# A graph layer followed by routed experts, one core: the gate computed from rows that are not yet normalised, and a routing table of tile and lane numbers in bf16

## The reference, cut to what matters

```python
x = x + gnn(layernorm(x), ...)                 # 3125 rows of 256
x_flat = layernorm(x)
gate_logits = x_flat @ Wg + bg + bias          # 8 experts
topk_vals, topk_idx = top_k(gate_logits, 2)
topk_w = softmax(topk_vals)
h = relu(einsum('td,edh->teh', x_flat, W1) + b1)    # 256 -> 512
y = einsum('teh,ehd->ted', h, W2) + b2              # 512 -> 256
out = x + einsum('ted,te->td', y, combine)     # combine: the two weights in their experts' columns
```

## Time and profile before

| | us |
|---|---|
| median of 3 runs (1615.25 to 1617.7) | 1615.89 |
| the profiled execution's own time | 1618.14 |
| its span on the core | 1616.4 |
| TensorE busy in the span | 1404.1 |
| VectorE busy | 726.7 |
| GpSimd busy | 185.2 |

### The profile page before, as it was taken

How to read it: one execution, slowest core, us unless ns; L and a number is a source line. 1 busy time by engine, 2 the same in 40 slices (tenths; PEclk the granted TensorE clock), 3 DMA queues, 4 the chain that set the end, 5 groups by cost and what they waited for, 6 DMA issues and landing times.

```text
span 1616.4 us, 25299 instructions
## 1 busy us (share of the span) xinstructions
PE 1404.1 (87%) x8992; PEld 855.5 (53%) x8993; DVE 726.7 (45%) x1676; ACT 389.9 (24%) x1040; POOL 185.2 (11%) x156
## 2 busy tenths in 40 slices
PE   2565578898869999999999999999999953899996
PEld 1554344444434554447444554447444532899995
DVE  6989777777741432213131232214112266343342
ACT  1320254344330420103001130104001031244342
POOL 1000200000000000000000000000000002477774
PEclk9886779999989999999999999999999976899998
DMA  5244000000000000000000000000003092244443
GB/s 114 66 160 157 1 1 1 1 2 1 1 20 1 13 2 0 1 0 14 0 1 0 14 1 0 1 1 7 1 1 80 0 314 83 40 69 70 68 74 43
DMA packets 49431, 57.82 MB, mean 36 GB/s; under 512 B 14201, under 2 KB 41483, under 8 KB 49066
## 3 DMA queue, kind: packets, MB, share of 16 engines
q1 hardware_dynamic: 38570, 41.67, 8.6%
q0 software_dynamic: 10752, 14.69, 5.7%
HBM read 42.36 MB, written 13.99 MB: 35 GB/s over the span
## 4 chain that ended last, share of the span: by engine, by line
PE 77%; DVE 11%; ACT 4%; issue 3%; DVEq 1%; DMA 1%; POOL 1%; SPq 0%; POOLq 0%
PE bank L904 40%; PE bank L994 8%; PE bank L1452 6%; PE bank L1462 6%; PE bank L830 4%; PE bank L2059 3%; ACT at L1925 3%; PE bank L2001 2%; DVE ohL L1723 1%; PE bank L910 1%; PE bank L2057 1%; PE bank L1443 1%; ACT m L851 1%; DVE ohS L1832 1%; PE bank L1417 1%
## 5 line engine op out<-in xcount | busy, mean ns | idle before, releaser
L904 PE MATMUL bank<-at,m 125*128 125x500 fp8e4 (+1 forms) x3500 | 691.1, 355 | 11.7 <-DVE aggT L918 6.1
L904 PEld LDWEIGHTS bank<-at,m 125*128 125x128 f16 x3500 | 318.4, 98 | 374.9 <-issue 58.2
L920 DVE SCALAR_TENSOR_TENSOR aggT<-bank,dnL,dinvB 128x500 f32<-128x500 f32 (+1 forms) x56 | 38.2, 683 | 458.1 <-PE bank L910 458.1
L1452 PEld LDWEIGHTS bank<-xtT,w1c 128*128 128x128 f32 x896 | 109.8, 194 | 2.8
L1452 PE MATMUL bank<-xtT,w1c 128*128 128x128 f32 x896 | 110.0, 277 | 0.0
L1179 POOL TENSOR_TENSOR idJ<-idJ,wts 125x1400 f32<-125x1400 f32 x2 | 8.0, 4008 | 863.5 <-DVE idJ L1335 863.5
L1462 PE MATMUL bank<-w2s,h1T 128*128 x448 | 106.1, 380 | 0.1
L1195 POOL DMA_INDIRECT out_rows<-ytb,rowS x56 | 96.8, 1729 | 51.7 <-issue 24.3
L1462 PEld LDWEIGHTS bank<-w2s,h1T 128*128 128x128 f32 x448 | 80.8, 190 | 9.3 <-issue 0.3
L1016 ACT ACTIVATE hB<-aggT,prm 128x500 f32<-128x500 f32 (+1 forms) x28 | 18.7, 667 | 266.7 <-DVE aggT L1060 266.7
L2059 PE MATMUL bank<-cnt,ohS 128*128 128x250 bf16 x504 | 77.6, 302 | 0.0
(11 more groups left out here) (367 smaller groups left out, 1619.0 us busy)
## 6 DMA issues: line engine op xcount, KB each, us to landing
slrow<-sl_dram SPq DMA_DIRECT2D x26, 512.0 KB, 4.9
w1s<-in_L_ffn_W SPq DMA_DIRECT2D x1, 4096.0 KB, 14.5
w2s<-in_L_ffn_W SPq DMA_DIRECT2D x1, 4096.0 KB, 18.6
xin<-in_x SPq DMA_DIRECT2D x1, 2800.0 KB
out_rows<-x SPq DMA_DIRECT2D x1, 2800.0 KB
xn_dram<-xn SPq DMA_DIRECT2D x1, 2800.0 KB
x<-in_x SPq DMA_DIRECT2D x2, 1344.0 KB
dinvB<-dinv_dram SPq DMA_DIRECT2D x1, 1562.5 KB
```

The lines of the kernel that those rows point to most:

```text
L904: pe.matmul(agg_bank(l, g)[:, 0:w], m[:, s, k, h * 128:(h + 1) * 128], at_block(q)[:, s, :], start=s == 0 and k == 0, stop=False)
L1452: last = pe.matmul(bank[4 + u][:, k * TT:(k + 1) * TT], w1c[:, u, h, k * 128:(k + 1) * 128], xtT[:, u, h, :], start=h == 0, stop=h == H - 1)
```

## The change

It touches six things.

1. **Gate from x2.** TensorE transposes tiles of `x2`, before they are normalised, and multiplies each with `wgs`, now with the transposed tile as the stationary operand and the 8 columns of `wgs` moving. The logits come out with rows on partitions. Another matmul gives the column sums of `wgs` (`csW`). VectorE corrects the logits: (raw - mean * csW) * rstd + bias. The stream of TensorE waits for `s_fw` at its start.
2. **Statistics in halves.** `back_dve` adds four tiles in one instruction, and statistics are taken of each half of 128 elements. Those of the first half move to the last graph layer.
3. **xn by ScalarE.** ScalarE writes the normalised rows, with the softmax's exponential after the tenth. SyncE stores `xn` ahead of `x2`, in two DMAs.
4. **Slot table in bf16.** Lane (0 to 124) and 128 times the tile number, both exact in bf16, replace the row number. A third table holds plain ones, from which `used` tells which choice fills a slot. `xn_dram` has 128 rows for each tile of 125, so that tile and lane give the row directly.
5. **Weights with the rows.** A row of `xn` has 258 elements: 256 and the two softmax weights. After each gather VectorE picks the weight of the tile's slots by two operations of 128x1 (`select`), and the next gather into the buffer waits for it.
6. **Tile numbers by GpSimd.** `te` and `ts` are worked out in 13 GpSimd instructions instead of 8 of VectorE.

```diff
         def back_dve(dve, j, t):
...
-            dve.tensor_tensor(x2[:, t, part], x2[:, t, part], row_slot(j, t), ALU.add).then_inc(s_lo, 1)
+            n = set_of(t).stop - t
+            rows = bank[ROWS_AT + (j * SETS_T + t // PER) % 3][0:P, 0:n * 128].rearrange("p (t d) -> p t d", d=128)
+            dve.tensor_tensor(x2[:, set_of(t), part], x2[:, set_of(t), part], rows, ALU.add).then_inc(s_lo, n)
...
         def experts_sp(sp):
...
+            sp.wait_ge(s_wx, 1)
+            for a, b in X_STORES:
+                sp.wait_ge(s_fn, b)
+                sp.dma_start(xn_dram.rearrange("(t p) d -> p t d", p=TT)[:, a:b, :], xn[:, a:b, :]).then_inc(s_xnd, 16)
             sp.wait_ge(s_lo, NT * (L + 2))
...
         def experts_pool(pool, step):
...
-                step(pool.tensor_tensor(idJ[:, n, :, 1, :], byJ, wts[:, 2 - n, :].unsqueeze(2).to_broadcast([P, NT, J]), ALU.mult))
-                pool.tensor_tensor(byJ, byJ, iotaN[:, :].unsqueeze(2).to_broadcast([P, NT, J]), ALU.mult).then_inc(s_tabP, 1)
+            pool.memset(xn[96:TT, :, :], 0.0).then_inc(s_cst, 1)
+            pool.wait_ge(s_ends, 1)
+            done_at, before_at = cmpJ[:, 0, :, :], cmpJ[:, 1, :, :]
+            step(pool.tensor_tensor(done_at, nte[0:1, 2, :].unsqueeze(1).to_broadcast([1, J, NE]),
+                                    iotaJ[0:1, :].unsqueeze(2).to_broadcast([1, J, NE]), ALU.subtract))
+            step(pool.tensor_scalar(done_at, done_at, 0.5, None, ALU.is_lt))
+            step(pool.tensor_tensor(before_at, done_at, nte[0:1, 1, :].unsqueeze(1).to_broadcast([1, J, NE]), ALU.mult))
+            for n in (4, 2):
+                step(pool.tensor_tensor(cmpJ[:, :, :, 0:n], cmpJ[:, :, :, 0:n], cmpJ[:, :, :, n:2 * n], ALU.add))
...
+            pool.tensor_scalar(te[:, :], teF[:, :], float(NE - 1), None, ALU.min).then_inc(s_slot, 1)
...
                     pool.wait_ge(s_xtT, j + 1)
+                    pool.wait_ge(s_sel, j + 1)
                     gather(j + XB)
...
         def experts_act(act):
...
+                act.activation(turned_x(t), bank[t % 4][:, 0:H * P].rearrange("p (h n) -> p h n", h=H), ACT.Copy).then_inc(s_gTe, 1)
...
+                if t == EXP_AT:
+                    act.wait_ge(s_ex, 1)
+                    act.activation(wts[:, 1, :], wts[:, 0, :], ACT.Exp).then_inc(s_exd, 1)
+                act.activation(xn[0:P, t, 0:D], x2[:, t, :], ACT.Identity, scale=frs[:, t:t + 1], bias=fnm[:, t:t + 1]).then_inc(s_fn, 1)
...
         def experts_dve(dve, step, rounded, inverse_root):
...
+            dve.wait_ge(s_gate, 1)
+            step(dve.tensor_copy(csW[:, :], GATE[0:P, NT * NE:(NT + 1) * NE]))
+            step(dve.tensor_tensor(lga[:, :, :], by_node(fmv[:, :, 0]), by_expert(csW[:, :]), ALU.mult))
+            step(dve.tensor_tensor(lga[:, :, :], GATE[0:P, 0:NT * NE].rearrange("p (t e) -> p t e", e=NE), lga[:, :, :], ALU.subtract))
             dve.wait_ge(s_fsd, 1)
             inverse_root(frs[:, :], fve[:, :], fsd[:, :], ft1[:, :])
...
-            for t in range(NT):
-                dve.tensor_scalar(xn[:, t, :], x2[:, t, :], fmv[:, t, 0:1], frs[:, t:t + 1], ALU.subtract, ALU.mult).then_inc(s_fn, 1)
...
+            step(dve.tensor_tensor(idJ[:, 2, :, :, :], to_tiles(iotaJ2[:, :, :], NT), by_pair(slt16[:, :, :], J), ALU.is_equal))
+            dve.tensor_scalar(idJ[:, 1, :, :, :], idJ[:, 2, :, :, :], iotaQ[0:P, :], None, ALU.mult)
+            dve.tensor_tensor(idJ[:, 0, :, :, :], idJ[:, 2, :, :, :], by_pair(tile_at[:, :, :], J), ALU.mult).then_inc(s_R, 1)
+            for a, b in R_PIECES:
+                dve.tensor_tensor(ohR[:, a:b, :, :], to_tiles(iotaT[:, :, :], b - a), by_pair(slp16[:, a:b, :], TT), ALU.is_equal).then_inc(s_R, 1)
...
+            def select(j, k, gathered):
+                dve.wait_ge(s_xt[k], gathered)
+                col = bass.ds(j, 1)
+                dve.tensor_tensor(wone[:, col], xtb[:, k, D:D + 1], used[:, 0, col], ALU.mult).then_inc(s_yt, 1)
+                dve.wait_ge(s_yt, j + 1)
+                dve.scalar_tensor_tensor(wS[:, col], xtb[:, k, D + 1:D + 2], used[:, 1, col], wone[:, col], ALU.mult, ALU.add).then_inc(s_sel, 1)
...
         def experts_pe(pe):
...
+            def gate(t):
+                pe.wait_ge(s_gTe, t + 1)
                 for h in range(H):
+                    last = pe.matmul(GATE[0:P, t * NE:(t + 1) * NE], turned_x(t)[:, h, :], wgs[:, h, :], start=h == 0, stop=h == H - 1)
                 last.then_inc(s_gl, 1)
...
+            pe.wait_ge(s_fw, FW)
+            pe.wait_ge(s_agge, H * NQ * L)
...
+            for s in range(SETS_T):
+                if s:
+                    for t in range(PER * (s - 1), PER * s):
+                        gate(t)
+                for t in tiles:
+                    turn_x(t)
+                for t in range(PER * (s + 3), min(PER * (s + 4), NT)):
+                    row_pe(pe, 1, t)
```

298 lines of the change are left out of this document (156 added, 142 removed).

## The result

The changed kernel takes 1594.45 us in the median of four runs (1591.81 to 1596.52), against 1616.49 (1615.25 to 1617.7) before: a ratio of 0.9863, 95% interval 0.9845 to 0.9881. The forecast was 1592, with a range of 1585 to 1605. The profiled execution took 1591.81 us, its span 1590.0.

The account below looks back on a forecast made before the run. TensorE bounds the expert loop, which stays; the gain comes from the 93.2 us ahead of it. 4.1 + 28.0 + 31.0 + 6.3 = 69.4 us, 23.8 less: 1594.3 profiled, 1592 as median, range 1585 to 1605.

Parts of the forecast that it names:

- The start, plus 4.1: TensorE's first transpose waits for s_fw, last the loads of b1: 4.1 us lost, bounds 2.9 to 5.4.
- The gate, 28.0: From TensorE's first transpose to the gate's end: 28.0 us instead of 43.9, from transposes, gate instructions and column sums.
- with the clock back up after the first few microseconds: Gate's stage: TensorE's clock recovers early, so the 25 transposes of hB take 4.5 us.
- Rival (b): Gate's small products don't overlap their loads: a pass costs 0.25 us instead of 0.13, plus 12, total 1604; 12%.
- 0.2 us or more: Sign that the prediction is wrong: gate passes on TensorE taking this long, where 0.13 us each was forecast.
- Gate to table, 31.0: From the gate's end to the finished slot table: 31.0 us instead of 42.97.
- The lock between VectorE and GpSimd: Behind s_ends, GpSimd's tile numbers and VectorE's operations block each other: plus 3.7 us, between 0 and 6.4.
- Table to first product, 6.3: From the table to the first expert product: 6.3 us, as in the kernel before.
- hidden, 5 us to spare: Store of x2 ends by 1362, GpSimd asks for it at 1367 behind four gathers, so it costs nothing.
- Rival (d): Stores come last, if ScalarE or SyncE is 8 us later than thought: 1597 with 5 us of loss; 4%.
- The loop: Expert loop set by TensorE, unchanged at 3.73 us for each of 56 tiles, with `select` hidden.
- Rival (e): GpSimd bounds the loop if longer rows make a gather 2.0 us: 1621 to 1631; 7%, plus 5% for a milder form.

Follow-up runs that it names:

- e1: Changed kernel with TensorE's wait for s_fw and the column sums moved from ahead of the first transpose to behind the first transposes: 1589.67 us, ratio 0.9844.
- e2: Changed kernel with the tile numbers te and ts moved back from GpSimd to VectorE, as eight operations: 1595.25 us, ratio 0.9875.
- e3: Changed kernel with SyncE storing x2 and the zero rows ahead of xn: 1590.01 us, ratio 0.984.
- e6: Changed kernel without the selection of each slot's softmax weight and GpSimd's wait for it: 1594.85 us, ratio 0.9869.
- e5b: Changed kernel with twenty-four 512-column products of zeros on TensorE ahead of the loop: 1588.25 us, ratio 0.9826.
- e7: Changed kernel with one addition per tile again and the first half's statistics back behind the last layer: 1596.23 us, ratio 0.988.
- e4: Changed kernel with a 256-column product of zeros behind each tile's gate products on TensorE: 1591.29 us, ratio 0.9843.

## Why the prediction was right, step by step

The mechanisms held, and the total of the four stages was off by 0.3 us only because a table that came out 1.7 too dear stood against a last stage 1.8 too cheap. That is luck. The median's 2.45 us above 1592 are the loop's 1.7 and the 0.6 by which four runs of the kernel before lie above the three that the forecast had (1616.49, 1615.89).

- **The start, plus 4.1.** TensorE's first instruction came 3.6 us later than before and its first transpose 4.6, on both sides of the value and inside 2.9 to 5.4. A DMA of b1 released it. e1 shows that it was loss and nothing else.
- **The gate, 28.0.** It took 28.63, and the sum was better than its terms. The transposes came out right, 4.6 us for the 25 of hB (I had 4.5) and 8.4 for the 50 of x2 (8.3), the latter as a mix of two speeds, 0.11 each at the full clock and 0.21 at the half. A gate pass, put at 0.13 from the earlier trace rows, costs 0.10 at the full clock and 0.20 at the half, 15.1 us for 104 where I had 13.5. The 1.7 for the last tile and the first sets at the low clock came to some 0.5. The step at fault is "with the clock back up after the first few microseconds": it came back and fell again at 1313, and no rival had that. Rival (b) named 0.25 for each pass but for another reason, loads that nothing covers; at the full clock a pass takes 0.10 us with its load. My mark "0.2 us or more" for being wrong did appear, in 39 of the 104 passes.
- **Gate to table, 31.0.** 29.33. The counts stood at 10.6 us (10.8 forecast). The lock between VectorE and GpSimd cost 2.0 us ahead of the tables and 0.3 in the four pieces of ohR (4.03 against 3.69 us in e2) instead of 3.7, inside 0 to 6.4: GpSimd's instructions stretched four small ones of VectorE, while those on 200 elements kept their 0.37. GpSimd paid too: its operations on 56 elements took 0.3 to 1.5 us, so the 0.15 us that I added for each instruction, which no row shows, was too little, and te came 14.3 us after `s_ends` instead of 11, still hidden. The mis-sized part is which of VectorE's operations lose: I had counted those with two SBUF inputs. L1368, L1370 and L1372 have two, ran beside GpSimd and took 0.36 to 0.37 us with and without it; the four stretched ones are three tensor_scalar and a CAST, with one tensor as input. The Trainium skill, page "SBUF — State Buffer", section "Who interferes with whom", names both kinds, copies, casts and tensor_scalar in their faster modes too. The rows here agree for those, and show next to no loss of VectorE's for the others (none on 200 elements, under 0.1 us in each table), though the long f32 comparisons of the kernel before did lose beside GpSimd (4.1 against 1.9 us). TensorE's products took 4.83 us (4.7).
- **Table to first product, 6.3.** 8.12, the one step that was wrong in kind. I checked x2's store against GpSimd's first *wait* for it and called it "hidden, 5 us to spare". It needs no wait to cost time: it had the DMA engines busy for 0.75 of the stretch in which the first gathers ran (the fourth window above), against 0.19 in the earlier trace rows. Measured from the first gather's issue the second landing is 1.3 us later than before (5.93, 4.61), and the transposes, which now stand behind both landings, add 0.5. Moving the store away brings back 1.6 and 0.5 (e3). Rival (d), stores that come last, had 4% and was closest to what happened, by x2 instead of xn.
- **The loop.** 3.73 us a tile as before (products of later tiles start at 1371.12, 1374.85, 1378.58), the selection hidden (e6), a gather 1.03 us against 1.01 in the earlier trace rows. Rival (e), GpSimd as the bound, is refuted: a row of 1032 bytes costs 0.02 us more a gather. The missing term is the clock at its start, plus 1.5 for the first 32 products, since TensorE now waits 5.8 us ahead of them at a landing that comes late; e5b, which fills this wait, has them at 3.84.
- **VectorE is no longer the bound of the gate.** So it is, with 9 to 10 us to spare (e7).

Three things stay open: what in TensorE's stream from 1303 to 1313 lets the clock fall (e4 shows only that with its products the clock stays up); where in the graph layers the end A gets its scatter of 6 us; and what parts 1, 3 and 4 are worth each. They bring most of the gain, 15.3 us in the gate's stage and 13.6 behind it, and no run here takes one of them back as a whole: their shares rest on the stage times and on the rows.

## What to carry to other kernels

When a transfer moves off the wait that names it, ask what else uses the DMA engines at that time: here a store with 5 us to spare by its semaphore set when the first gathers landed, and the last 0.9 us or more of the table's gain were lost behind it. Once an engine's busy share is full, look at its clock by the microsecond before you cut its work: 25 useless products made the gate 4 us shorter, and 24 ahead of the loop took 2.5 us off its first 32 products. Test each part of a large change alone when it has run, since here the tile numbers on GpSimd and the wide additions with the early statistics gained nothing.
